# Peeling the last two expert tiles and scaling four elements of the final norm transposed

## The reference

```
h   = gelu(einsum('td,edf->etf', xf, w1) + b1)          # per expert, f = 1024
eo  = einsum('etf,efd->etd', h, w2) + b2
out = einsum('etd,te->td', eo, combine)                  # two experts per position
x   = layernorm(x + out, ln3_g, ln3_b)                   # (x - mean) * rstd * g + b
```

## Time and profile before

| What | us |
|---|---|
| median of three runs | 1194.17 |
| profiled execution, its own time | 1193.72 |
| its span (first to last instruction) | 1192.0 |
| TensorE busy over the span | 1067.3 (90%) |
| VectorE busy | 850.7 (71%) |
| ScalarE busy | 767.9 (64%) |
| GpSimd busy | 521.1 (44%) |
| last matmul ends about | 1150 |
| last additions have landed | 1163.8 |

### The profile page before, as it was taken

The page is one execution under the profiler, slowest core; times in us unless marked ns, Lnnn a source line. Parts: engine busy times, 40 slices in busy tenths (PEclk is TensorE's granted clock), DMA queues, the critical chain, the costliest instruction groups (busy, mean ns, idle before and its releaser), DMA issues. The chain is left out here.

```text
span 1192.0 us, 28185 instructions
## 1 busy us (share of the span) xinstructions
PE 1067.3 (90%) x9419; PEld 899.8 (75%) x9419; DVE 850.7 (71%) x2558; ACT 767.9 (64%) x1607; POOL 521.1 (44%) x736
## 2 busy tenths in 40 slices
PE   7788888889999999999989989988989999999950
PEld 6466656668888888886767667766789999999950
DVE  2777888877766666667767677674548887888846
ACT  4365576667766666656556665655458988988932
POOL 4355556423222213445667246542423545354544
PEclk9799999999999999999999999999989999999985
DMA  8656756755355444355756856651647777787764
GB/s 165 97 83 156 87 99 97 97 73 77 51 64 90 55 59 55 64 98 97 110 75 103 131 108 99 101 89 42 255 143 230 239 231 241 225 252 230 242 163 145
DMA packets 112047, 152.43 MB, mean 128 GB/s; under 512 B 23233, under 2 KB 95425, under 8 KB 105537
## 3 DMA queue, kind: packets, MB, share of 16 engines
q1 hardware_dynamic: 101712, 138.64, 55.0%
q0 software_dynamic: 8352, 10.80, 4.7%
q10 hardware_dynamic: 1872, 1.60, 1.1%
HBM read 78.39 MB, written 21.62 MB: 84 GB/s over the span
## 5 line engine op out<-in xcount | busy, mean ns | idle before, releaser
L1091 ACT ACTIVATE probs<-s 128x384 f32<-128x384 f32 (+1 forms) x512 | 264.6, 540 | 140.8 <-PE s L839 130.6
L1173 DVE TENSOR_REDUCE neg_max<-s 128x2 f32<-128x512 f32 x256 | 168.8, 689 | 66.6 <-PE s L811 59.7
L839 PE MATMUL s<-q_stack,k_stack 98*128 98x256 bf16 (+1 forms) x1024 | 175.8, 261 | 20.1 <-ACT probs L1091 18.6
L670 POOL TENSOR_SCALAR_AFFINE_SELECT probs<-probs 128x256 f32<-128x256 f32 x256 | 105.8, 422 | 166.1 <-ACT probs L1091 165.5
L1170 DVE CUSTOM_DVE_ANT_0 s<-s,mask_qk 128x256 f32<-128x256 f32 x256 | 114.6, 447 | 54.6 <-PE s L808 44.3
L839 PEld LDWEIGHTS s<-q_stack,k_stack 98*128 98x128 bf16 x1024 | 88.6, 99 | 47.8 <-ACT probs L1091 31.7
L861 PE MATMUL pv<-probs,v 128*32 128x256 f32 (+1 forms) x2048 | 110.1, 355 | 1.7 <-POOL probs L670 1.4
L1583 PE MATMUL moe<-rows_hi,e_w_hi 128*128 128x256 f32 x368 | 103.2, 281 | 2.2 <-DVE rows_lo L1700 2.2
L1583 PE MATMUL moe<-e_w_hi,e_hidden_hi 128*128 128x256 f32 x368 | 104.6, 284 | 0.0
L1704 DVE TENSOR_TENSOR e_hidden_lo<-e_hidden,e_hidden_hi 128x512 fp32r<-128x512 f32 x92 | 77.5, 842 | 37.0 <-ACT e_hidden_hi L1665 36.0
L1583 PE MATMUL moe<-e_w_lo,e_hidden_hi 128*128 128x256 f32 x368 | 102.8, 279 | 0.0
(11 more groups left out here) (241 smaller groups left out, 3013.2 us busy)
## 6 DMA issues: line engine op xcount, KB each, us to landing
w<-in_expert_w SPq DMA_DIRECT2D x26, 1024.0 KB, 5.2
k_stack<-k_part SPq DMA_DIRECT2D x192, 128.0 KB, 4.3
q_stack<-q_part SPq DMA_DIRECT2D x180, 128.0 KB, 5.9
w_next<-in_expert_w SPq DMA_DIRECT2D x22, 1024.0 KB, 5.3
rows<-slots_x SPq DMA_DIRECT2D x25, 256.0 KB, 2.7
slots_x<-filler SPq DMA_DIRECT2D x8, 518.0 KB, 4.5
cT<-in_context SPq DMA_DIRECT2D x16, 256.0 KB, 6.3
e_b<-in_expert_b SPq DMA_DIRECT2D x24, 128.0 KB
```

Of the source, the lines that this page charges most:

```text
L670: pool.affine_select(out=blocks, in_=blocks, compare_op=ALU.is_ge, fill=0.0, base=0, pattern=[[0, TILES], [1, P]], channel_multiplier=-1). ...
L839: last = pe.matmul(dst[:, kt * S:kt * S + S - q0], k[:, kt * P:(kt + 1) * P], q[:, q0:S], start=True, stop=True)
L1091: act.activation(probs_of(n, hd)[:, 0:width], s2[hd % 2][:, 0:width], ACT.Exp, scale=SCALE).then_inc(probs_ready, 1)
L1173: dve.tensor_reduce(neg_max[:, :, hd], src[:].rearrange("p (t s) -> p t s", t=TILES), AX_X, ALU.max, negate=True).then_inc(s1_free, 1)
```

## The change

The loop makes ten turns in place of eleven (`LOOPED = PAIRS - 1`). Tiles 21 and 22 are written out behind it on every engine:

- TensorE: `up(21)`, `turn(22)`, `down(20)`, `down(21)`, `up(22)`, `down(22)`; `down(21)` stands ahead of `up(22)`, and `turn(23)` is gone. `down(22)` is "apart": each 128 rows have a bank and a signal of their own.
- SyncE: the fetches for tiles 23 and 24 are gone, and the loads of gain and shift are no longer behind them. A small load `columns` is new (gain and shift as columns, 128 x 4).
- ScalarE and VectorE: the first weights of tile 23 are not split. The second weights of tile 22 are split before its hidden quarters are halved.
- GpSimd, tile 22: the share product is made for each 128 rows as soon as its half of the result is there, then comes the wait for the additions of tile 21.
- Final norm: the groups are elements (0), (1), (2, 3), (4, 5), (6, 7) and the offset of a group is computed behind the moments of the first element of the next one. Elements 2 to 5 are transposed by TensorE (four 128 x 128 transposes) into PSUM, scaled and shifted there by ScalarE with per-partition columns, transposed back by TensorE, and copied out of PSUM by VectorE. GpSimd applies the gain of elements 0, 1 and 6; VectorE that of 7. The shift of 0, 1, 6 and 7 is VectorE's.

```
-        GAIN_BY_DVE = (3, 6)
+        LOOPED = PAIRS - 1
+        TURNED = (2, 3, 4, 5)
+        GAIN_BY_POOL = (0, 1, 6)
+        GROUPS = ((0,), (1,), (2, 3), (4, 5), (6, 7))
...
-            with sp.Fori(0, PAIRS) as j:
+            with sp.Fori(0, LOOPED) as j:
...
+            last_e = expert(last_tile)
+            sp.wait_ge(result_ready, last_tile - 1)
+            fetch_bias(last_e, 0)
+            sp.dma_start(columns[:], t["end_columns"]).then_inc(norm_loaded, 16)
...
-            add_rows(last_tile, 0, PAIRS + 1)
+            add_rows(last_tile - 2, 0, PAIRS)
+            add_rows(last_tile - 1, 1, PAIRS + 1)
+
+            pool.wait_ge(row_data_ready, last_tile + 1)
+            for m in range(GT):
+                pool.wait_ge(result_ready, last_tile + 1 + m)
+                pool.sem_inc(gate, 1)
+                pool.tensor_tensor(result[0][:, m, :], result[0][:, m, :], share[0][:, m:m + 1].to_broadcast([P, D]), ALU.mult)
+            pool.wait_ge(added[1], ADDED * (PAIRS + 1))
+            pool.sem_inc(gate, 1)
+            pool.tensor_copy(token[0][:], token_next[0][:]).then_inc(row_data_taken, 1)
+            pool.drain()
+            for m in range(GT):
+                pool.indirect_dma_start(x_rows, bass.IndirectOffsetOnAxis(ap=token[0][:, m:m + 1], axis=0), result[0][:, m, :], None, compute_op=ALU.add).then_inc(added[0], 16)
...
             inverse_root(0)
             inverse_root(1)
             gain_of(0)
             inverse_root(2)
             gain_of(1)
             inverse_root(3)
-            gain_of(2)
-            for b in range(3, B):
-                if b not in GAIN_BY_DVE:
-                    gain_of(b)
+            inverse_root(4)
+            gain_of(6)
...
-            down(last_tile, 0)
+            up(last_tile - 1, 1)
+            turn(last_tile, 0, PAIRS + 1)
+            down(last_tile - 2, 0)
+            down(last_tile - 1, 1)
+            up(last_tile, 0)
+            down(last_tile, 0, apart=True)
+
+            def turn_rows(u):
+                b = TURNED[u]
+                pe.wait_ge(normal_ready, b + 1)
+                for k in range(KC):
+                    for m in range(TILES):
+                        last = pe.transpose(up_bank[u][:, k * TILES * P + m * P:k * TILES * P + (m + 1) * P], z[b][:, m, k * P:(k + 1) * P], ident[:])
+                last.then_inc(z_turned, 1)
+
+            def turn_back(u):
+                pe.wait_ge(z_scaled, u + 1)
+                ...
+            for u in range(0, len(TURNED), 2):
+                turn_rows(u)
+                turn_rows(u + 1)
+                turn_back(u)
+                turn_back(u + 1)
...
+            act.wait_ge(norm_loaded, 16 * 3)
+            for b in range(4):
+                normal(b)
+            scale_turned(0)
+            scale_turned(1)
+            for b in range(4, 6):
+                normal(b)
+            scale_turned(2)
+            scale_turned(3)
+            for b in range(6, B):
+                normal(b)
...
+            for q in range(QUARTERS):
+                second_low(last_tile - 1, 1, q)
+            row_data(1, last_tile - 1, PAIRS)
+            add_bias(last_tile - 2, 0, PAIRS)
+            for q in range(QUARTERS):
+                second_low(last_tile, 0, q)
+            row_data(0, last_tile, PAIRS + 1)
+            add_bias(last_tile - 1, 1, PAIRS)
+            for q in range(QUARTERS):
+                hidden_low(last_tile, 0, q)
+            add_bias_apart()
...
+            def variances(g):
+                some = slice(GROUPS[g][0] * TILES, (GROUPS[g][-1] + 1) * TILES)
+                for b in GROUPS[g]:
+                    moments(b)
+                    if b == GROUPS[g][0] and g > 0:
+                        offset_of(g - 1)
+                dve.drain()
+                dve.tensor_scalar(var_eps[:, some], mean_var[:, some, 1], EPS, None, ALU.add).then_inc(var_ready, 1)
...
+            def take_back(u):
+                dve.wait_ge(z_back, u + 1)
+                dve.tensor_copy(z[TURNED[u]][:].rearrange("p t d -> p (t d)"), back_bank[u][:]).then_inc(y_ready, 1)
+
+            for g in range(len(GROUPS)):
+                variances(g)
+            shift_of(0)
+            shift_of(1)
+            offset_of(len(GROUPS) - 1)
+            for b in ENDED[2:]:
+                if b in TURNED:
+                    take_back(TURNED.index(b))
+                else:
+                    shift_of(b)
```

More of the change, by code:

```diff
@@ L1362, in moe_part @@
         shift = sb("ln3_shift", [P, D])
+        columns = sb("ln3_columns", [P, 2 * KC])
+        turned = [sb(f"turned{u}", [P, KC, TILES * P]) for u in range(4)]
         w1 = [w1_first[0], w1_next[0]]
@@ L1584, in pair_products, with up @@
                 return last
-            def up(n, i, quarters=range(QUARTERS)):
+            def up(n, i, quarters=range(QUARTERS), first=False):
                 if quarters[0] == 0:
@@ L1619, in _ @@
             idle(WARM_HALVES)
-            up(0, 0, range(0, 2))
+            up(0, 0, range(0, 2), first=True)
             turn(1, 1, 1)
-            up(0, 0, range(2, QUARTERS))
-            with pe.Fori(0, PAIRS) as j:
+            up(0, 0, range(2, QUARTERS), first=True)
+            with pe.Fori(0, LOOPED) as j:
                 for i in (1, 0):
@@ L1669, in _ @@
             rows_high(0, 0)
-            step(0, 0, 1, range(0, 2))
+            step(0, 0, 1, range(0, 2), first=True)
             rows_high(1, 1)
-            step(0, 0, 1, range(2, QUARTERS))
-            with act.Fori(0, PAIRS) as j:
+            step(0, 0, 1, range(2, QUARTERS), first=True)
+            with act.Fori(0, LOOPED) as j:
                 for i in (1, 0):
@@ L1685, in _, with scale_turned @@
                 last.then_inc(normal_ready, 1)
+            def scale_turned(u):
+                act.wait_ge(z_turned, u + 1)
+                for k in range(KC):
+                    last = act.activation(turned[u][:, k, :], up_bank[u][:, k * TILES * P:(k + 1) * TILES * P], ACT.Identity, scale=columns[:, k:k + 1], bias=columns[:, KC + k:KC + k + 1])
+                last.then_inc(z_scaled, 1)
+            act.wait_ge(norm_loaded, 16 * 3)
[9 more added lines that the diff above has]
+                normal(b)
         @block.vector
@@ L1724, in add_bias, with add_bias_apart @@
                 dve.tensor_tensor(result[i][:], down_bank[i][:].rearrange("p (g d) -> p g d", g=GT), b2_e[i][:].unsqueeze(1).to_broadcast([P, GT, D]), ALU.add).then_inc(result_ready, 1)
+            def add_bias_apart():
+                dve.wait_ge(b2_loaded[0], 16 * (PAIRS + 1))
+                dve.wait_ge(added[0], ADDED * (PAIRS + 1))
+                for m in range(GT):
+                    dve.wait_ge(down_full, last_tile + 1 + m)
+                    dve.tensor_tensor(result[0][:, m, :], (turn_bank[1] if m else down_bank[0])[:, m * D:(m + 1) * D], b2_e[0][:], ALU.add).then_inc(result_ready, 1)
             dve.sem_inc(w1_lo_ready, QUARTERS)
@@ L1734, in _ @@
             row_data(0, None, 1)
-            with dve.Fori(0, PAIRS) as j:
+            with dve.Fori(0, LOOPED) as j:
                 for i in (1, 0):
@@ L1773, in shift_of @@
             def shift_of(b):
-                if b in GAIN_BY_DVE:
+                if b in GAIN_BY_POOL:
+                    dve.wait_ge(gained, GAIN_BY_POOL.index(b) + 1)
+                else:
                     gain_of(b)
-                else:
[L1777 to L1788, removed]
+                dve.tensor_tensor(z[b][:], z[b][:], shift[:].unsqueeze(1).to_broadcast([P, TILES, D]), ALU.add).then_inc(y_ready, 1)
+            def take_back(u):
+                dve.wait_ge(z_back, u + 1)
+                dve.tensor_copy(z[TURNED[u]][:].rearrange("p t d -> p (t d)"), back_bank[u][:]).then_inc(y_ready, 1)
+            dve.wait_ge(norm_loaded, 16 * 3)
+            for g in range(len(GROUPS)):
[6 more added lines that the diff above has]
+                    take_back(TURNED.index(b))
+                else:
+                    shift_of(b)
 _OUT = ((B, S, D), "float32")
```

82 lines of the change are left out of this document (48 added, 34 removed).

## The result

The changed kernel takes 1187.69 us (median of 5 runs, 1185.73 to 1190.6) against 1194.17; the ratio is 0.9947 with a 95% interval of 0.9931 to 0.9964. Measured again later it was 1187.25 against 1194.58, 0.9944 (0.9928 to 0.996). So it is 6.5 to 7.3 us faster. The prediction said 1189.4 in a range of 1186.0 to 1193.0: direction and range held, and the size was 1.7 short.

What follows compares the result with a forecast made beforehand. The bound was a chain: TensorE until `down(22)` is done, then GpSimd's product and additions waiting on earlier landings, then the final norm. Additions 4.4 plus norm 0.2 gave 4.6 gained, forecast 1189.4 us, 8-in-10 range 1186.0 to 1193.0.

Steps and rivals of the forecast that it cites:

- mechanism of the additions: Last tiles on GpSimd: each tile's additions wait for the previous landing, the share product lies under it; 4.4 us gained.
- rival of slow landings: Additions of the last tiles: each landing stays at 5.82 us though weight fetches are gone; 1.8 gained, 1192.4; chance 0.17.
- L20: Landing of tile 20's additions: 1144.58 if quiet, 1146.70 beside the loads of gain and shift; 1146.0 taken.
- L20 to L21: Tile 20's landing to tile 21's: copy at +0.13, first issue 0.96 later, second 1.88 later, landing 3.70 later; 6.67 in all.
- price of its company: GpSimd's issues of tile 21 beside VectorE's low halves: 1.99 in place of 1.58, so 0.4 an issue; left in the range.
- stronger lock: GpSimd's issues: a VectorE operation taking both ports locks GpSimd out, up to 0.69 an issue, 1.4 for two; time 1190.8.
- L21 to L22: Tile 21's landing to tile 22's: copy, two issues and a landing again, 6.67; from 1152.7 to 1159.4.
- slower rival: Behind the loop: engines entering code not yet run stall 3.06 each on three engines; 4.6 slower, 1198.8; chance 0.05.
- first meeting: Norm: VectorE's offset of element 1, reached at t = 7.4, waits for GpSimd's gain of element 0, ending about 8.5.
- my s: Norm: time after the first load of z when ScalarE starts element 2; 12.1, half a us either way.
- second meeting: Norm: VectorE's offset of elements 2 and 3 waits for GpSimd's gain of element 1, until t = 12.4; over 1 us long.
- no meeting in the norm: Norm: offsets slip in ahead of the gains, ScalarE starts at 10.2, norm gains 2.0; sum 6.4, 1187.7; chance 0.2.

Runs made afterwards that it cites:

- another edit alone: The kernel before with the loads of gain and shift issued ahead of the loop in place of behind it; 1191.82 us, ratio 0.998.
- gain and shift early, changed: The changed kernel with the loads of gain and shift ahead of the loop; 31.9 us from `turn(22)` to the first load of z, norm 23.2.

## Why the prediction was right, and where it was short

The mechanism of the additions was right: the share product lies under the landing of tile 21, `down(21)` is there early, and the loads of gain and shift are away from tile 21. Undone one at a time, the product ahead of the wait is worth 1.1 to 1.3; the order of `down(21)` 1.9 to 2.1; the rest of 4.9 to 5.8 is the landing of tile 21, 5.8 to 6.1 before and 3.7 to 3.8 after, which another edit alone gives back in the kernel before (1.7 to 2.4). These were taken from different kernels and overlap, so they need not add up exactly. I had said 4.4 for all. The rival of slow landings falls, with 4.2, 3.8 and 3.8 for the three tiles.

- L20: I took the issues of tile 20 as unmoved and its landing 5.1 behind the second one. Counted from `turn(22)`, the second issue was at 13.7 (14.3 before; the copy of tokens ahead of it took 0.19 for 0.71) and the landing took 4.2. L20 came at 17.9 where I had 19.4. Counted on from `turn(22)` in the profile of before that is 1144.5, ahead of the 1145 that I had named as a sign of being wrong. I had set the collision with gain and shift between quiet and full; 1.8 ahead of the addition they cost 0.2 over the 4.0 that tile 20 took without them.
- L20 to L21 was 7.4 and not 6.67. The copy took 0.37 and the first issue 2.07 for 1.58, and began 1.15 behind the copy's start for 0.96; the landing took 3.8 for 3.7. VectorE's low halves lay beside copy and issue. That is the price of its company that I had left in the range; the stronger lock by the Trainium skill (SBUF — State Buffer, "DVE blocks DMA") would have allowed 0.69 an issue, and the trace shows 0.49.
- L21 to L22 was 6.95 and not 6.67: the issue began 1.11 behind the copy's start, for 0.96, and the landing took 3.8 for 3.7.
- These errors have opposite signs: L20 was forecast 1.5 too late, and the two steps behind it 0.75 and 0.3 too short. That they leave only 0.5 is luck.
- `down(22)`: a gap of 0.49 on TensorE for a forecast of 0.2 to 0.5. No engine stood idle on its own code behind the loop; the slower rival had nothing to it. (The 0.4 for `turn(23)` isn't half of 1.11, which is 0.56; nothing hangs on it.)

The term that was mis-sized most is the norm: 0.2 forecast, 2.05 in the first two profiles, 0.8 to 1.2 once the late load of element 2 is taken out (24.1 and 24.4 for the old code in two profiles without a wait for it, 23.2 and 23.3 for the new). The step that failed is the first meeting, that of element 1's offset with the gain of element 0. I had the moments of element 2 begin at t = 6.33, because I had taken one late load for the rule. They began at 5.72, so the offset started at 6.70, 0.11 ahead of the gain at 6.81, and didn't wait. The run with `down(21)` behind shows that it is this load: there element 2 was late (6.43), the meeting took place, and the norm took 24.8, with the same code and the same short powers (23.1 to 23.4 in the six other profiles of this norm). In all nine other profiles with the new groups element 2 was in time and the offset went first. The power of two values took 0.69 to 0.73, where I had only the row of 1.04 for four; this moved the start of the whole but didn't decide the race. ScalarE's start in earnest, my s, was 10.5 and not 12.1, and my own steps would even have given 12.4, the end of the offset (2, 3). From s to the end I had 13.1, and it took 12.8. The second meeting and ScalarE as the bound were as forecast, and moving one gain took the second meeting away for 0.9 to 1.0. The transposes ran at the lower clock level at first (0.50), but not to the end (0.73). ScalarE did wait for them, 0.23 twice: I had counted 0.2 and 0.3 of such waits in the sum and still named a wait as a sign of being wrong.

The rival "no meeting in the norm" had the number (1187.7), but not the reason: one meeting of the two took place, and the additions gave more than its 4.4. Both of my terms, 4.4 and 0.2, were too small, so nothing cancelled between them: the forecast was short by 1.7, and the time lies in the range because the range was wide enough, at 3.4 and 3.6 to either side.

## What to carry to other kernels

A chain of dependent transfers is paid by what lands beside it: look for small loads that nobody wants yet (gain and shift here, 2 us in the kernel before) and issue them long before. Where two engines race within a tenth of a microsecond and the loser waits 1.2, work out the order for each possible outcome, and move the work that isn't urgent away from the race; one moved line brought 0.9 to 1.0 of the norm. And a profile is one execution: a wait in it that depends on a load is a sample until a second profile has it too. Where such a wait decides a race, work out the forecast with it and without it.

## What the runs showed of the hardware

- An operation of VectorE on 4 values a partition took 0.13 to 0.17 us where it met no gain of GpSimd, and 1.21 to 1.22 when a gain of 1.26 had begun 0.06 to 0.07 before it, in every one of the profiles with such a meeting. On 2 values it took 0.83 when it began 0.45 behind the gain (`down(21)` behind `up(22)`), and 0.13 when it began 0.11 ahead of it. In each of these meetings it ended 0.02 to 0.03 behind the gain's end.
- GpSimd's power took 0.69 to 0.73 for two values a partition and 1.01 to 1.05 for four, 1.38 to 1.45 with VectorE's shifts beside it.
- GpSimd's issue of an indirect addition took 2.02 to 2.08 where a low half of 0.69 on VectorE had begun 0.07 to 0.13 ahead of it, and 1.58 where one began 0.70 behind its start (gain and shift early, changed), as with VectorE idle.
- An indirect addition of 128 rows landed 3.7 to 4.0 behind its issue in the quiet; 4.4 beside loads of 1 MB, one or the other of which was in flight throughout; and beside the two loads of 128 KB for gain and shift, 4.2 to 4.8 when the first was issued 1.5 to 1.8 ahead of it, 4.0 to 4.1 when 1.6 behind, and 5.8 to 6.1 when 1.0 to 1.4 behind.
